# Expert tiles: the next tile's transposes behind the second block of the second layer

## What is computed

```python
combine = gw[:, :, None] * ew
y = jnp.zeros_like(xf)
for g in range(G):
    h = jax.nn.gelu(jnp.einsum('nd,edm->enm', xf, W1[g]) + b1[g][:, None, :], approximate=False)
    o = jnp.einsum('enm,emd->end', h, W2[g]) + b2[g][:, None, :]
    y = y + jnp.einsum('end,ne->nd', o, combine[:, g, :])
```

## Time and profile before

| | us |
|---|---|
| median of 3 runs | 786.02 |
| lowest and highest | 785.11, 786.42 |
| span of the profiled execution | 782.1 |
| median less that span | 3.9 |
| TensorE busy in the span | 672.5 (86%) |
| VectorE, ScalarE, GpSimd busy | 426.2, 236.5, 323.5 |

### The profile page before, as it was taken

The page is one execution under the profiler, slowest core; times in us unless marked ns, Lnnn a source line. Parts: engine busy times, 40 slices in busy tenths (PEclk is TensorE's granted clock), DMA queues, the critical chain, the costliest instruction groups (busy, mean ns, idle before and its releaser), DMA issues.

```text
span 782.1 us, 19902 instructions
## 1 busy us (share of the span) xinstructions
PE 672.5 (86%) x6348; PEld 571.2 (73%) x6348; DVE 426.2 (55%) x1247; ACT 236.5 (30%) x673; POOL 323.5 (41%) x265
## 2 busy tenths in 40 slices
PE   5957858898989996863379899999999999999995
PEld 5724646656745885753269789999999999999994
DVE  7574583745479559977934344444444434434342
ACT  3112312123247211111433333333343333333331
POOL 4730730011023322520334456555564655655554
PEclk9976968577999998975579999999999999999998
DMA  9900000000000030013116765464545665565432
GB/s 349 255 2 3 3 3 2 3 1 3 1 1 1 1 122 1 1 68 132 30 31 164 217 170 116 119 182 81 164 113 161 172 169 161 115 163 114 103 50 38
DMA packets 34982, 70.05 MB, mean 90 GB/s; under 512 B 6353, under 2 KB 21234, under 8 KB 34930
## 3 DMA queue, kind: packets, MB, share of 16 engines
q0 software_dynamic: 15840, 17.71, 13.5%
q10 hardware_dynamic: 8064, 33.12, 12.6%
q1 hardware_dynamic: 11026, 18.48, 7.3%
HBM read 59.31 MB, written 9.98 MB: 89 GB/s over the span
## 4 chain that ended last, share of the span: by engine, by line
PE 62%; DVE 17%; DMA 6%; issue 4%; POOL 1%; ACTq 1%; ACT 1%; DVEq 0%; POOLq 0%
PE bank L1492 17%; PE bank L1484 12%; PE bank L1487 7%; PE bank L1340 4%; PE bank L1469 3%; PE bank L1272 3%; PE bank L1292 3%; DMA arena<-normed_rows,fetch_u 3%; PE bank L1356 2%; DMA out_dram<-arena,number_u 2%; PE bank L1310 1%; PE bank L1283 1%; DVE zx L894 1%; DVE arena L1097 1%; DVE arena L1094 1%
## 5 line engine op out<-in xcount | busy, mean ns | idle before, releaser
L631 POOL DMA_INDIRECT out_dram<-arena,number_u x80 | 127.0, 1587 | 51.6 <-DMA out_dram<-arena,number_u 26.3
L625 POOL DMA_INDIRECT arena<-normed_rows,fetch_u x80 | 78.3, 979 | 114.9 <-DMA out_dram<-arena,number_u 51.0
L1179 DVE COPY arena<-bank 128x256 f32<-128x256 f32 x81 | 34.4, 425 | 119.5 <-PE bank L1469 110.8
L796 ACT ACTIVATE arena<-bank,arena 128x128 f32<-128x128 f32 x234 | 64.5, 375 | 115.5 <-PE bank L1487 115.5
L1492 PE MATMUL bank<-arena 128*128 128x192 f32 x468 | 83.0, 326 | 0.1
L1492 PEld LDWEIGHTS bank<-arena 128*128 128x128 f32 x468 | 75.4, 190 | 0.5 <-ACT arena L796 0.5
L1197 DVE TENSOR_SCALAR arena<-bank,arena 128x192 f32 x80 | 33.4, 418 | 59.1 <-PE bank L1492 57.5
L533 POOL TENSOR_SCALAR rstd<-mv 128x4 f32<-128x4 f32 x12 | 2.7, 229 | 147.5 <-DVE mv L883 147.5
L1484 PE MATMUL bank<-arena 128*128 128x128 f32 x468 | 59.1, 276 | 1.4 <-DVE arena L1179 1.1
L1484 PEld LDWEIGHTS bank<-arena 128*128 128x128 f32 x468 | 56.9, 192 | 3.0 <-issue 1.5
L796 ACT ACTIVATE arena<-bank,w_space 128x128 f32<-128x128 f32 x132 | 36.5, 375 | 67.0 <-PE bank L1487 67.0
(11 more groups left out here) (241 smaller groups left out, 1263.8 us busy)
## 6 DMA issues: line engine op xcount, KB each, us to landing
arena<-in_moe_w_dram ACTq DMA_DIRECT2D x14, 579.0 KB, 6.1
arena<-in_moe_w_dram ACTq DMA_DIRECT2D x14, 576.0 KB, 4.2
arena<-in_xf_dram SPq DMA_DIRECT2D x8, 512.0 KB, 9.8
w_space<-in_moe_w_dram ACTq DMA_DIRECT2D x7, 579.0 KB, 5.8
w2small<-in_moe_w_dram ACTq DMA_DIRECT2D x7, 579.0 KB, 5.6
w_space<-in_moe_w_dram ACTq DMA_DIRECT2D x7, 576.0 KB, 4.2
wab<-in_moe_w_dram ACTq DMA_DIRECT2D x7, 576.0 KB, 4.3
arena<-in_w_dram SPq DMA_DIRECT2D x8, 480.0 KB, 9.1
```

Source lines behind the costliest of these rows:

```text
L625: pool.indirect_dma_start(out=mo_stage[:, s * ROWN:(s + 1) * ROWN], out_offset=None, in_=normed_rows, in_offset=bass.IndirectOffsetOnAxis( ...
L631: pool.indirect_dma_start(out=out, out_offset=bass.IndirectOffsetOnAxis(ap=number_u[:, s:s + 1], axis=0), in_=mo_res[:, s * D:(s + 1) * D] ...
L796: nc.scalar.activation(mo_hT[:, m, :], bank[2 + m][:, 0:P], ACT.Gelu, bias=b1[:, m:m + 1]).then_inc(free[2 + m], 1)
L1179: nc.vector.tensor_copy(mo_xT.rearrange("p k t -> p (k t)"), bank[1][:, 0:2 * P]).then_inc(free[1], 1)
```

## The change

The call `transpose_rows(i + 1)` moves from between the two layers into the second layer's loop, behind the product of block m = 1. The lines behind it move up by one: L1491 and L1492 become L1490 and L1491.

```diff
                     for m in range(MC):
                         r, c = m % 2 * REST, HID + m // 2 * P
                         mm(bank[2 + m][:, 0:P], w1e[r:r + REST, c:c + P], mo_xT[r:r + REST, 1, :], start=False, stop=True).then_inc(full[2 + m], 1)
-                    transpose_rows(i + 1)
                     pe.wait_ge(free[0], i + moe_base[0])
                     for m in range(MC):
                         pe.wait_ge(free[2 + m], i + (moe_base[2 + m] + 1))
                         ins = mm(bank[0][:, 0:D], mo_hT[:, m, :], w2e[:, m, :], start=(m == 0), stop=(m == MC - 1))
+                        if m == 1:
+                            transpose_rows(i + 1)
                     ins.then_inc(full[0], 1)
```

## The result

| | before | after |
|---|---|---|
| median of the runs | 785.57 us (785.06 to 786.42, 4 runs) | 810.13 us (806.96 to 811.61, 4 runs) |
| ratio to before, 95% interval | 1 | 1.0313 (1.0268 to 1.0359) |
| profiled execution, its span | 782.1 us | 811.55 us, 809.7 us |

The kernel became 24.6 us slower where I had said 8.6, so the time lies far outside my range of 789 to 799. The sign was right and the size was a third of it.

The account below looks back on a forecast made before the run. TensorE was taken to bound the last 69 tiles, GpSimd's transfers the first 11. Terms 6.8 + 0.9 + 0 + 0.9 = +8.6 us on 786.0 gave 794.6 us, range 789.0 to 799.0.

Parts of the forecast that it names:

- TensorE's own sum: Expert stage: a tile takes 3.21 us behind B, its first L1487, against 3.09; 57 tiles pay 6.8 us.
- The stall for Gelu: Second layer's first weight load waits for the first Gelu until B + 0.94 (B: first L1487), a new 0.08 us per tile.
- the exposed load: Second layer's first weight load has nothing to hide under: 0.10 us, where a transpose's load cost 0.06 us.
- the free changes between product and transpose: Transposes inside the second layer: switching from product to transpose and back costs nothing; upper bound 0.15 us.
- the 0.12 us a tile: Steady tiles of the expert stage: each gets 0.12 us longer; 57 tiles pay it, 6.8 us.
- The first 11 tiles: Before 455 us, where GpSimd's transfers bound: later transposes shift this part by 0.9 us, ends 0 and 1.3.
- VectorE as the next wait: VectorE's copy L1179 after the transposes: starts later, but the next tile's L1484 still has 0.6 us to spare.
- L1179 starts at B + 2.12 everywhere: Expected profile: VectorE's copy starts 2.12 us behind B, the tile's first L1487, in all tiles.
- GpSimd's chain becomes late: Rival: fetches allowed 0.77 us later, result-buffer waits outgrow the spare 0.6 us; +3 to +4, 797 to 799 us; 13%.
- No stall for Gelu: Rival: second layer's first load doesn't wait for Gelu, a tile costs only 0.04 us; +3.2, 789.2 us; 8%.
- transposes not free: Rival: switching between product and transpose costs 0.15 us more in each of 61 tiles; +9.2, 804 us; 6%.
- faster: Rival: the transposes' exposed load goes away and nothing new is exposed; 3.4 us gained less 0.9, 783.5 us; 3%.

Follow-up runs that it names:

- e1_no_add: The changed kernel without GpSimd's L631, the adding of a tile's result to the output, and its two waits; 788.17 us.
- e1_no_add_before: The kernel before, without L631 (the adding of a tile's result to the output) and its two waits; 779.67 us.
- e7_after_again: The changed kernel run again unchanged, on the same chip as a repeat of the kernel before (784.57 us); 809.85 us.
- experiment 4: The changed kernel, but GpSimd begins L631 only once L1179 has taken the next transposes; ratio 1.0112 (1.0072 to 1.0151) to the kernel before.

## Why the prediction was wrong

**Right: TensorE's own sum.** The stall for Gelu (0.94), the exposed load, the free changes between product and transpose and the 0.12 us a tile all stand in the first timeline. The pair without L631 gives +8.6 us over the tiles, and the kernel with L631 moved stands +8.8 us above the old one. The first 11 tiles are part of it: 53.2 us in e1_no_add, 51.8 in e1_no_add_before, +1.4 where I had 0.9 with 1.3 as the upper end.

**Wrong: "VectorE as the next wait".** I took 0.04 us from the transposes' record to L1179 and wrote "L1179 starts at B + 2.12 everywhere", with 0.6 us to spare. It starts there in 15 of the 80. In 61 the signal is held, mostly until about L631's end; in 55 L1179 comes later than the latest B + 2.7, at about B + 3.1 as a rule, and each such tile takes TensorE's 4.65 us no longer but the loop's 5.1 us. That is 24.4 us against 4.7 for the old order in the same places, so 19.7 us that my sum didn't have; 8.6 + 19.7 = 28.3, of which the profiled executions show 27.6 and the medians 24.6. The size of the second term depends on the trace of the old order that is taken: 368.3 us is from the one without a late signal, the two later ones have 371.6 and 372.5. The pair from one chip, 397.0 us in e7_after_again against 371.6, gives 25.4 over the tiles, beside 25.3 between their times, and leaves 16.8 for this step.

**Why I couldn't read it off, and what I could have.** The trace of before holds no late signal at all, so the 1 us had no row; two later profiles of the same kernel have plenty. But the exposure was readable. In the old order L1179 starts at B + 1.35 where nothing is late and is needed by 3.09 - 0.48 = B + 2.61: 1.3 us to spare, in which a lateness of 1 us vanishes. The new order left 0.6. I priced the move of the signal by 0.77 us only at its own value, against a margin of 0.6 us for which I had one value from quiet tiles. And I didn't lay the loop L1179, L1195, L625, L631 (about 5.1 us) beside a tile's 4.65: before, the loop went through L1179 only when something was late, and recovered. After the change it seldom does, since behind a late L1179 the transposes' end falls into the next L631 again.

**The rivals.** "GpSimd's chain becomes late" (797 to 799, 13%) was nearest: the late fetch, L625 behind L1195, is there, 85.0 us of waits. Its mechanism wasn't: the wait for the result buffer at L1201 didn't grow, it shrank from 10.3 us in the late tiles alone to 1.8 in all. "No stall for Gelu" and "transposes not free" are refuted by the first timeline, "faster" by everything.

## What to carry to other kernels

A wait that costs nothing has a margin, and a move spends it. When a signal moves later, lay the whole loop that hangs on it (through the other engines and back) beside the period of the engine that bounds, and ask what happens if one link is 1 us late: does the next turn recover, or does it find the same link late again? The gate of experiment 4 shows the remedy: take the overlap away, here by starting the transfer behind the copy, rather than making a link faster. And one profile of a kernel in which something is never late is no evidence that it can't be: take more than one.

## What the runs showed of the hardware

TensorE's semaphore updates can be held while GpSimd makes the descriptors of an indirect DMA. It happened for transposes, for 64-row and for 128-row products, in 11 of the 12 profiles in which a signal fell into such an L631 at all, in 69 of 75 cases in the changed kernel, when the 1.59 us L631 began 0.30 us (in a few cases up to 0.5) behind the 0.98 us L625. Of the 447 updates held close behind L625, 30 came 0.6 to 0.84 us into L631 and the others 1.3 to 1.8 us into it, most of them at 1.5 to 1.7. With over 0.55 us between the transfers it was 10 of 615. ScalarE's and VectorE's updates were never late: the latest came 0.013 us behind its record's end. The Trainium skill, Perfetto Trace Analysis, section DMA Instruction — SWDGE (GPSIMD), says that such a row ends when the last of GpSimd's processors has written its descriptors, and not with the transfer. This case's rows agree: in the late tile shown first the held update came at 525.62, where L631's row ends, and the first landing of L631's transfer followed at 527.17.

Open stays what does the holding, why TensorE's updates alone are hit, and why the first profile of the kernel before shows none in 46 cases. That profile is odd in one more way: it holds 476 of ScalarE's 480 updates in these tiles, the other twelve hold 342 to 443, and TensorE's are as incomplete, so the table counts those that were recorded. Whether the recording has to do with the holding, no run tells. The rule of the 0.55 us is read from 13 profiles and from one experiment in which the period changed as well. A short pause also means that L625's own transfer runs while L631 is made ready: its packets moved from 0.70 to 1.31 us behind L625's row in the changed kernel (medians), and from 0.71 to 1.30 in the kernel before. Pauses of 0.55 to 1.25 us let the two overlap in part, and none of 154 signals was late with them, but no run tells the two apart. So the rule is well supported and not isolated. No run delayed a signal of TensorE's in the old order by other means than GpSimd's.
